# Layer 0 of a two-layer graph network: VectorE keeps a round's destinations and second harmonic in a PSUM bank

## The chip, the cores and the metric

One core of one Trainium2 chip. The metric is device time in microseconds (us) of one execution of the whole program, as a median of runs; lower is better. Engine names are those of the profile: PE is TensorE, DVE is VectorE, ACT is ScalarE, POOL is GpSimd, SP is SyncE. L653 is line 653 of the kernel before.

## The reference

Two message-passing layers over 6250 nodes and 206250 edges (sorted by destination), each followed by a residual sum and a layer norm. The change touches the edge part of the first layer only.

```python
# layer 0, for every edge e = (src, dst); es: 1 harmonic, ev: 3 harmonics
xs_e, xv_e = xs[src], xv[src]                       # gather by source
out_s = (einsum(xs_e * es, W_ss) / sqrt(64) + einsum(xv_e, ev, W_vv) * ISQ3 / sqrt(32)) * ISQ2
out_v = (einsum(xs_e, ev, W_sv) * ISQ3 / sqrt(64) + einsum(xv_e, es, W_vs) * ISQ3 / sqrt(32)) * ISQ2
messages = concat(out_s, out_v) * sigmoid(edge_scalars @ W_rad.T + b_rad)
agg = segment_sum(messages, dst, num_segments=n)    # scatter by destination
h = x + agg
...
x = layernorm(x + concat(hs @ L_s, hv @ L_v))
x = layernorm(x + second_layer(x, ...))             # another edge layer, not changed here
```

All products by the weights of layer 0 are made once per node into a table of 448 columns, so that an edge needs one gathered row, a few products by its four harmonics, sums of parts, one product by the radial part, and the scatter.

## The kernel before

**Stages.** The program makes the table of layer 0, runs edge layer 0 (about 77 to 2460 us of the profiled execution), works on the nodes, runs edge layer 1 (about 2590 to 5044 us), and norms the result. In both edge layers the edges go by in 403 supertiles of 512 edges (4 columns, TPS, of 128 edges, one to a partition). Four supertiles (SLOTS) are a round; there are 101 rounds. On each engine a loop runs over the rounds and holds the code of four supertiles; the first and the last round stand outside it.

**One supertile of layer 0, by engine.** Each engine runs its own list of instructions in order; semaphores tie them.

- POOL issues four indirect DMAs (L373), one per column; each reads 128 source numbers out of SBUF (srcs) and gathers 128 table rows into one of four slots of rows0. A slot is filled again once ACT (semaphore s_wtd) and DVE (s_wone) have used its rows.
- ACT waits for the rows, weights two parts of them by harmonics 3 and 0 (L470, eight instructions, scale from the tile harm), copies harmonics from dst_sh to harm every other supertile (L445), and makes the sigmoid of the radial product in PSUM (L498).
- DVE (function supertile): weights a third part by harmonic 1 (weight_by_one, L653, which waits for ACT's s_whead), adds a fourth part by harmonic 2 in four instructions (L660, the last of which waits for PE's sums of two supertiles ago), adds the finished sums of two supertiles ago to the node array (add_sums, L719), makes the one-hot matrix of the destinations against the current window of 128 nodes (select, L712), sums parts (L679 twice, the second waits for ACT's sigmoid) and multiplies by the radial part (L685, from PSUM). Where edges reach into a further window of nodes (444 one-hots for 401 supertiles in the stretch) it makes another one-hot and another sum (further, L739).
- PE multiplies one-hot by messages (sums, L967) into banks 4 to 6 and makes the radial product of the supertile after next (radial0, L947) into banks 0 to 3.

**Order and queues.** Between rounds DVE branches back (L785) and loads the round's windows from SBUF into registers (windows_of, L776) before it can form the addresses of the next round's instructions. Small register instructions of DVE's sequencer (named DVEq in the profile) stand between the others; they keep the engine waiting only where the sequencer has not run ahead of it. The tile dst_sh holds, for two chunks of four rounds, 16 columns of destinations and harmonics per supertile; SP reloads a chunk when DVE is through with it (s_add), so data for the next round lies there long before.

The two instructions that the change touches, and the wait at a round's start:

```python
nc.vector.tensor_tensor(u[:, :, 384:480], r[:, :, 352:448], by(1), ALU.mult)                    # L653, by(1) is a view of harm
return nc.vector.tensor_tensor(onehot[:, b, :, :], bc(iota[...], 1, [P, TPS, P]),              # L712
                               bc(dst, 2, [P, TPS, P]), ALU.is_equal)                           # dst is a view of dst_sh
if j == 0: dve.wait_ge(s_dsh[l], (i // CHUNK + 1) * 16)                                         # L755
```

Of the kernel before, what the change touches and what calls it, by code (L numbers as in the profile page):

```python
# [10 lines left out]
P = 128  # L11
TPS = 4
SUP_EDGES = TPS * P
SLOTS = 4
# [10 lines left out]
CHUNK = 4  # L25
# [29 lines left out]
def mk_gnn_resnorm_d2_gnn_r8_694f30_kernel(nc, a):  # L55
    f32, bf16, i32, i16 = mybir.dt.float32, mybir.dt.bfloat16, mybir.dt.int32, mybir.dt.int16
    ALU = mybir.AluOpType
# [3 lines left out]
    with ctx:  # L61
# [3 lines left out]
        def sem(name):  # L65
            return ctx.enter_context(nc.semaphore(name))
# [7 lines left out]
        at = SLOTS * TPS * ROW0  # L74
# [70 lines left out]
        def bank(b, n=1):  # L145
            return ps[:, b * BANK:(b + n) * BANK]
# [6 lines left out]
        wps = [two_to_a_bank(2 * b, 192) for b in range(2)]  # L153
        FIRST, MORE = 4, 6
        hps = bank(7)
        fps = [bank(6), bank(7)]

        def of_node(j, b=0, n=DIM):
# [31 lines left out]
        s_msg = [sem(f"messages_made{l}") for l in range(2)]  # L190
        s_wtd = [sem(f"rows_weighted{l}") for l in range(2)]
        s_whead = sem("scalar_parts_weighted")
        s_wone = [sem(f"rows_weighted_by_dve{l}") for l in range(2)]
        s_part = [sem(f"message_part{l}") for l in range(2)]
        s_both = sem("message_both_parts")
# [405 lines left out]
        def _(dve):  # L601
# [40 lines left out]
            def bc(x, axis, shape):  # L642
                return x.unsqueeze(axis).to_broadcast(shape)

            def weight_by_one(l, s, i, j, opens):

                def by(k):
                    return harm[:, j, :].rearrange("p (t k) -> p t k", k=4)[:, :, k:k + 1].to_broadcast([P, TPS, 96])

                if l == 0:  # L650
                    dve.wait_ge(s_whead, s + 1)
                    u, r = weighted0[:, j % DEEP0, :, :], rows0[:, j, :, :]
                    nc.vector.tensor_tensor(u[:, :, 384:480], r[:, :, 352:448], by(1), ALU.mult)  # L653
                    for t in range(TPS):
                        if t == 1:
                            dve.wait_ge(s_add[0], s + 1)
                        if t == TPS - 1 and not opens:
                            dve.wait_ge(s_agg[0], s + 1)
                        to = u[:, t, 128:224]
                        last = nc.vector.scalar_tensor_tensor(to, r[:, t, 0:96], harm[:, j, 4 * t + 2:4 * t + 3], to,  # L660
                                                              ALU.mult, ALU.add)
                else:
                    dve.wait_ge(s_wtd[1], s + 1)
                    u, r = weighted1[:, j % 2, :, :], rows1[:, j, :, :]
                    nc.vector.tensor_tensor(u[:, :, 352:448], r[:, :, 32:128], by(1), ALU.mult)  # L665
                    if not opens:
                        dve.wait_ge(s_agg[1], s + 1)
                    last = nc.vector.tensor_tensor(u[:, :, 448:544], r[:, :, 128:224], by(2), ALU.mult)  # L668
                last.then_inc(s_wone[l], 1)
# [35 lines left out]
                dve.wait_ge(s_both, s + 1)  # L705
                nc.vector.tensor_tensor(m[:, :, 64:96], h[:, :, 1, 0:MV], w[:, :, 160:192], ALU.mult).then_inc(s_msg[1], 1)  # L706

            def select(i, j, b, window):

                of_round = dst_sh[:, :, :].rearrange("p (q j) c -> p q j c", j=SLOTS)  # L710
                dst = of_round[:, bass.ds(i % (2 * CHUNK), 1), j, 0:TPS].rearrange("p o t -> p (o t)")
                return nc.vector.tensor_tensor(onehot[:, b, :, :], bc(iota[:, bass.ds(window * P, P)], 1, [P, TPS, P]),  # L712
                                               bc(dst, 2, [P, TPS, P]), ALU.is_equal)
# [7 lines left out]
            def edge_layer(l):  # L721
# [17 lines left out]
                def further(s, i, j, window, k):  # L739
# [7 lines left out]
                    at = dve.snap(window + k + 1).with_bounds(min_val=1, max_val=LAST)  # L747
                    dve.reg_mov(visit, e + 1)
                    dve.wait_ge(s_addx[l], next_visit())
                    select(i, j, 2, at).then_inc(s_ohx[l], 1)  # L750
                    dve.reg_mov(waiting_more, at)

                def supertile(s, i, j, windows, more, opens=False):
                    if j == 0:
                        dve.wait_ge(s_dsh[l], (i // CHUNK + 1) * 16)  # L755
                    weight_by_one(l, s, i, j, opens)
                    if opens:
# [4 lines left out]
                        add_sums(l, FIRST + j % 2, windows[j - 2] if j > 1 else held(of_last[j])).then_inc(s_add[l], 1)  # L762
                    if l == 0:
                        dve.wait_ge(s_wtd[0], s + 1)
                    select(i, j, j % 2, windows[j])
                    (messages0, messages1)[l](s, j)
                    with dve.If(more > 0):
                        further(s, i, j, windows[j], 0)
# [3 lines left out]
                    if j > 1:  # L772
                        dve.reg_mov(of_last[j - 2], windows[j])

                def windows_of(i):
                    return nc.values_load_multi_w_load_instructions(  # L776
                        wtab[0:1, bass.ds(i, 1), 0:2, :], engines=[dve.engine], min_val=0, max_val=LAST,
                        skip_runtime_bounds_check_because="a dst is a node's number, so its window is one of the tiles")[1]

                values = windows_of(0)  # L780
                for j in range(SLOTS):
                    if l == 0 and j == 2:
                        dve.wait_ge(s_acc0x, 16)
                    supertile(j, 0, j, values, values[SLOTS + j], opens=j < 2)
                with dve.Fori(1, ROUNDS - 1) as i:  # L785
                    values = windows_of(i)
                    for j in range(SLOTS):
                        supertile(i * SLOTS + j, i, j, values, values[SLOTS + j])
                values = windows_of(ROUNDS - 1)
                for j in range(LAST_SLOTS):  # L790
                    supertile((ROUNDS - 1) * SLOTS + j, ROUNDS - 1, j, values, values[SLOTS + j])
# [431 lines left out]
```

## Time and profile before

| what | value |
|---|---|
| median of 3 runs | 4607.15 us (4604.56 to 4610.92) |
| span of the profiled execution | 5144.5 us |
| edge layer 0 in it | 77 to 2460 us |
| edge layer 1 in it | 2590 to 5044 us |
| DVE busy, share of the span | 75% |
| POOL busy, share of the span | 67% |
| PE busy, share of the span | 83% |

The profiled execution is 537 us longer than the median run. Its page gives, for every engine, the time its instructions took and the idle time before them with what ended it; the chain of work is followed back from the last instruction through whatever released each step. Durations of neighbouring DVE instructions overlap a little, so the step from one start to the next is what an instruction costs in a row.

### The profile page before, as it was taken

To read this page: it belongs to the slowest core of one execution; us is meant where nothing else is said; L and a number is where in the kernel's file an instruction comes from. 1 tells how busy PE (TensorE), PEld (TensorE's weight loads), DVE (VectorE), ACT (ScalarE), POOL (GpSimd) and SP (SyncE) were. 2 spreads that over 40 slices of the span, in tenths; PEclk is the share of its full clock that TensorE was granted. 3 is DMA by queue.
4 is the path that set the end of the run, shared out by engine and by line. 5 is a ranking of instruction groups with operands and counts; after the bars stand their busy time and mean duration, and the time that the engine had idled before them with its cause. 6 is when DMAs were issued, how large, how long until landed. Compare 5 with 4: busy or idle time off the path is not lost.

```text
span 5144.5 us, 61111 instructions
## 1 busy us (share of the span) xinstructions
PE 4277.3 (83%) x12412; PEld 2600.5 (51%) x12413; DVE 3878.0 (75%) x8785; ACT 2612.5 (51%) x8195; POOL 3471.2 (67%) x3267
## 2 busy tenths in 40 slices
PE   6877877877877887887878888988988898888897
PEld 4555555555555555555644444444444444444445
DVE  5878877877878887887667777777777776777777
ACT  3545555545555555554544445545454454555554
POOL 4777777777777777777266666666666666666661
PEclk7555555555555555555889999999998899999999
DMA  7655565665565665656233333333333333333331
GB/s 250 167 166 160 166 171 159 166 169 160 167 168 161 168 167 164 168 162 166 85 85 88 84 86 84 87 82 86 87 86 82 84 84 83 87 86 85 85 86 52
DMA packets 245761, 640.14 MB, mean 124 GB/s; under 512 B 57085, under 2 KB 95407, under 8 KB 245627
## 3 DMA queue, kind: packets, MB, share of 16 engines
q0 software_dynamic: 181152, 556.66, 39.8%
q1 hardware_dynamic: 64576, 83.11, 5.3%
q8 instruction: 13, 0.21, 0.0%
q14 instruction: 20, 0.16, 0.0%
HBM read 618.66 MB, written 20.88 MB: 124 GB/s over the span
## 4 chain that ended last, share of the span: by engine, by line
DVE 34%; PE 27%; issue 16%; another core or an unknown queue 9%; ACT 6%; DVEq 4%; DMA 2%; POOL 2%; ACTq 0%; POOLq 0%; SPq 0%
PE ps L967 15%; DVE work L679 10%; PE ps L960 6%; DVE work L660 6%; DVE onehot L712 5%; ACT work L470 5%; PE ps L954 3%; DVE work L653 2%; DVE acc L719 2%; POOL arena L373 2%; DVE arena L719 1%; PE ps L947 1%; DVE work L699 1%; DVEq L776 1%
## 5 line engine op out<-in xcount | busy, mean ns | idle before, releaser
L373 POOL DMA_INDIRECT work<-table,srcs x1596 | 1639.5, 1027 | 796.7 <-issue 633.8
L373 POOL DMA_INDIRECT arena<-table,srcs x1596 | 1755.0, 1100 | 611.4 <-issue 516.3
L967 PE MATMUL ps<-arena,onehot 128*128 128x161 f32 x3608 | 1034.6, 464 | 507.4 <-DVE arena L685 264.4
L967 PE MATMUL ps<-work,onehot 128*128 128x384 f32 x3608 | 1345.2, 521 | 79.3 <-DVE work L706 59.1
L967 PEld LDWEIGHTS ps<-arena,onehot 128*128 128x128 f32 x3608 | 884.8, 308 | 830.3 <-issue 769.8
L470 ACT ACTIVATE work<-arena,harm 128x160 f32<-128x160 f32 (+1 forms) x3224 | 984.7, 389 | 301.0 <-DMA arena<-table,srcs 266.3
L470 ACT ACTIVATE work<-work,harm 128x96 f32<-128x96 f32 (+1 forms) x3224 | 1070.3, 415 | 22.2 <-DMA work<-table,lists 11.6
L967 PEld LDWEIGHTS ps<-work,onehot 128*128 128x128 f32 x3608 | 684.8, 199 | 631.8 <-issue 270.6
L947 PE MATMUL ps<-wrad,escal 49*128 49x320 f32 x1612 | 905.2, 707 | 0.0
L960 PE MATMUL ps<-fc,hid 128*128 128x384 f32 x1612 | 639.1, 522 | 219.2 <-ACT hid L560 124.5
L679 DVE TENSOR_REDUCE work<-work 128x256 f32<-128x768 f32 (+1 forms) x806 | 656.7, 853 | 149.6 <-ACT ps L498 85.4
L560 ACT ACTIVATE hid<-ps 128x256 f32<-128x256 f32 x403 | 153.6, 381 | 1182.3 <-remote 652.7
L498 ACT ACTIVATE ps<-ps 128x640 f32<-128x640 f32 x403 | 276.5, 686 | 824.2 <-issue 285.2
L712 DVE TENSOR_TENSOR onehot<-iota,dst_sh 128x512 f32 (+1 forms) x902 | 616.9, 684 | 15.5 <-issue 6.4
L947 PEld LDWEIGHTS ps<-wrad,escal 49*128 49x128 f32 x1612 | 427.7, 293 | 262.4 <-issue 247.8
L960 PEld LDWEIGHTS ps<-fc,hid 128*128 128x128 f32 x1612 | 315.4, 201 | 482.5 <-ACT hid L560 162.7
L660 DVE SCALAR_TENSOR_TENSOR work<-arena,harm,work 128x96 f32<-128x96 f32 x1612 | 405.9, 311 | 171.6 <-remote 137.3
L668 DVE TENSOR_TENSOR work<-work,harm 128x384 f32<-128x384 f32 x403 | 223.1, 554 | 322.0 <-remote 189.5
L665 DVE TENSOR_TENSOR work<-work,harm 128x384 f32<-128x384 f32 x403 | 223.7, 555 | 280.1 <-issue 146.5
L703 DVE TENSOR_TENSOR work<-work,ps 128x768 f32<-128x768 f32 x403 | 380.4, 944 | 0.0
L685 DVE TENSOR_TENSOR arena<-work,ps 128x640 f32<-128x640 f32 x403 | 330.8, 821 | 13.9
L653 DVE TENSOR_TENSOR work<-arena,harm 128x384 f32<-128x384 f32 x403 | 223.2, 554 | 152.8 <-issue 109.3
(127 smaller groups left out, 2503.9 us busy)
## 6 DMA issues: line engine op xcount, KB each, us to landing
escal<-in_escal SPq DMA_DIRECT2D x404, 98.0 KB
arena<-table,srcs POOLq DMA_INDIRECT x1596
work<-table,srcs POOLq DMA_INDIRECT x1596
table<-work SPq DMA_DIRECT2D x49, 224.0 KB, 4.6
dst_sh<-in_dst_sh SPq DMA_DIRECT2D x52, 160.0 KB
table<-work SPq DMA_DIRECT2D x7, 784.0 KB, 4.0
acc<-in_xd SPq DMA_DIRECT2D x1, 3920.0 KB
arena<-in_xd SPq DMA_DIRECT2D x7, 560.0 KB, 4.6
```

The costliest lines, as they stand in the source:

```text
L373: pool.indirect_dma_start(out=rows[:, j, t, :], out_offset=None, in_=table, in_offset=bass.IndirectOffsetOnAxis(ap=of[:, j, t:t + 1], axis ...
L470: last = nc.scalar.activation(u[:, t, to:to + c1 - c0], r[:, t, c0:c1], ACT.Copy, scale=harm[:, j, at:at + 1])
L498: nc.scalar.activation(rad[j % 2], rad[j % 2], ACT.Sigmoid).then_inc(s_act[0], 1)
L653: nc.vector.tensor_tensor(u[:, :, 384:480], r[:, :, 352:448], by(1), ALU.mult)
L660: last = nc.vector.scalar_tensor_tensor(to, r[:, t, 0:96], harm[:, j, 4 * t + 2:4 * t + 3], to, ALU.mult, ALU.add)
L679: return nc.vector.tensor_reduce(to, parts[:, :, :, 0:MS].rearrange("p t k c -> p t c k"), AX.X, ALU.add)
L685: nc.vector.tensor_tensor(m[:, :, 0:DIM], u[:, :, 0:DIM], c, ALU.mult).then_inc(s_msg[0], 1)
L703: nc.vector.tensor_tensor(blocks(m[:, :, 192:384], 3), blocks(u[:, :, 256:544], 3)[:, :, :, 0:MS], bc(w[:, :, 64:128], 2, [P, TPS, 3, MS]) ...
L712: return nc.vector.tensor_tensor(onehot[:, b, :, :], bc(iota[:, bass.ds(window * P, P)], 1, [P, TPS, P]), bc(dst, 2, [P, TPS, P]), ALU.is_ ...
L947: last = mm(rad[j % 2][:, 2 * k:2 * k + 2, :], escal[:, j, k * P:(k + 1) * P], wrad[:], start=True, stop=True)
L960: last = mm(wps[j % 2][:, 2 * k:2 * k + 2, :], hid[:, j % 2, k * P:(k + 1) * P], fc2[:], start=True, stop=True)
L967: last = mm(bank(to)[:, 0:(MSG0, MSG1)[l]], onehot[:, b, t, :], m[:, j % 2, t, :], start=t == 0, stop=t == TPS - 1)
```

## The change

In layer 0, DVE copies the 16 destinations (as floats) and the 16 second harmonics (harmonic 1) of each partition for the next round from dst_sh into two halves of PSUM bank 7, which nothing else uses in layer 0. It does so at the end of each round, before the loop's branch (and once before the first round). The one-hots, first and further, read the destination from there, and L653's product reads the harmonic from there. The wait for dst_sh at a round's start becomes a wait for these copies, and the wait for dst_sh moves in front of them. ACT's copies into harm stay, since L470 and L660 still use them. Layer 1 is as it was.

```diff
+        dst_ps = bank(7)[:, 0:2 * SLOTS * TPS].rearrange("p (b j t) -> p b j t", b=2, j=SLOTS)
+        harm_ps = bank(7)[:, 2 * SLOTS * TPS:4 * SLOTS * TPS].rearrange("p (b j t) -> p b j t", b=2, j=SLOTS)
...
+            def of_psum(x, i, j):
+                return x[:, bass.ds(i & 1, 1), j, :].rearrange("p o t -> p (o t)")
...
-                    nc.vector.tensor_tensor(u[:, :, 384:480], r[:, :, 352:448], by(1), ALU.mult)
+                    nc.vector.tensor_tensor(u[:, :, 384:480], r[:, :, 352:448], bc(of_psum(harm_ps, i, j), 2, [P, TPS, 96]), ALU.mult)
...
-            def select(i, j, b, window):
+            def hold(i):
+
+                of_round = dst_sh[:, :, :].rearrange("p (q j) c -> p q j c", j=SLOTS)[:, bass.ds(i % (2 * CHUNK), 1), :, :]
+                first = of_round.rearrange("p o j c -> p (o j) c")
+                nc.vector.tensor_copy(dst_ps[:, bass.ds(i & 1, 1)].rearrange("p o j t -> p (o j) t"), first[:, :, 0:TPS])
+                sh1 = first.bitcast(f32)[:, :, TPS:5 * TPS].rearrange("p j (t k) -> p j t k", k=4)[:, :, :, 1]
+                nc.vector.tensor_copy(harm_ps[:, bass.ds(i & 1, 1)].rearrange("p o j t -> p (o j) t"), sh1).then_inc(s_held, 1)
+
+            def select(l, i, j, b, window):
+
+                if l == 0:
+                    return nc.vector.tensor_tensor(onehot[:, b, :, :], bc(iota[:, bass.ds(window * P, P)], 1, [P, TPS, P]),
+                                                   bc(of_psum(dst_ps, i, j), 2, [P, TPS, P]), ALU.is_equal)
...
-                    if j == 0:
+                    if j == 0 and l == 0:
+                        dve.wait_ge(s_held, i + 1)
+                    if j == 0 and l == 1:
                         dve.wait_ge(s_dsh[l], (i // CHUNK + 1) * 16)
...
+                def hold_next(i):
+
+                    dve.wait_ge(s_dsh[0], ((i + 1) // CHUNK + 1) * 16)
+                    hold(i + 1)
...
                 with dve.Fori(1, ROUNDS - 1) as i:
                     values = windows_of(i)
                     for j in range(SLOTS):
                         supertile(i * SLOTS + j, i, j, values, values[SLOTS + j])
+                    if l == 0:
+                        hold_next(i)
```

The instructions of DVE move at two places. ISA and REGISTER_ALU are register instructions of its sequencer. The end of a round in the loop of layer 0, after the code for further windows, before the change:

```order
L751 ISA
L770 COMPARE_AND_BRANCH
L769 UNCONDITIONAL_BRANCH
L773 ISA
L785 COMPARE_AND_BRANCH
```

The same place after the change:

```order
L791 UNCONDITIONAL_BRANCH
L795 ISA
L720 ISA [waits dst_sh_loaded0]
L720 REGISTER_ALU
L720 ISA
L720 COPY ps<-dst_sh 128x16
L722 ISA
L722 COPY ps<-dst_sh 128x16
L817 REGISTER_ALU
L817 COMPARE_AND_BRANCH
```

Five sequencer instructions (three ISA and two REGISTER_ALU) and the two copies stand there more. The start of a round, from the branch back to the first product and what follows it, before the change:

```order
L785 ISA
L776 TENSOR_LOAD wtab
L755 ISA
L651 ISA [waits dst_sh_loaded0]
L653 TENSOR_TENSOR work<-arena,harm 128x4x96 [waits scalar_parts_weighted]
L660 SCALAR_TENSOR_TENSOR work<-arena,harm,work 128x96
```

And after it:

```order
L817 ISA
L803 TENSOR_LOAD wtab
L775 REGISTER_ALU
L659 ISA [waits dst_and_harmonic_in_psum]
L661 REGISTER_ALU [waits scalar_parts_weighted]
L661 ISA
L661 TENSOR_TENSOR work<-arena,ps 128x4x96
L668 SCALAR_TENSOR_TENSOR work<-arena,harm,work 128x96
```

The wait for dst_sh is gone from here, one for the copies stands in its place, and two more register instructions stand between the load of the windows and the product.

## Rows read from the trace of the kernel before

**Rows 1.** Stretches: us; busy us of PE, PEld, DVE, ACT, POOL; granted clock, DMA share.

```profile
77.00:2460.00 2383.00, 1883.98 (x5182) 1303.32 (x5183) 1899.85 (x4104) 1259.79 (x3915) 1764.27 (x1605) 0.57 0.60 167
2590.00:5044.00 2454.00, 2158.97 (x5971) 1115.63 (x5972) 1794.91 (x4090) 1225.30 (x3899) 1653.07 (x1610) 0.93 0.32 85
```

**Rows 2.** Chain that ended last, 1200 to 1500 us: shares; longest pieces (start, us, what).

```profile
by line: DVE work L679 22.7%; issue 21.5%; DVE work L660 13.2%; DVE onehot L712 8.8%; another core or an unknown queue 8.6%; DVE work L653 5.8%; DVE acc L719 4.1%; POOL arena L373 3.4%; DVEq L776 2.1%; DMA arena<-table,srcs 2.1%; ACT work L
...
1254.55 8.42 issue
1341.74 13.31 another core or an unknown queue
```

**Rows 3.** Waits, 77 to 2460 us: who waited for whom, us, times, longest.

```profile
DVE work L660 <- remote: 137.3, 24, 12.5
DVE work L653 <- issue: 109.3, 121, 3.9
...
DVE work L679 <- ACT ps L498: 85.4, 13, 9.1
...
DVE work L653 <- ACT work L470: 30.7, 25, 12.7
```

**Rows 4.** Groups, 77 to 2460 us: line engine op tiles shapes xcount | busy, mean ns | idle.

```profile
L373 POOL DMA_INDIRECT arena<-table,srcs x1596 | 1755.0, 1100 | 611.4 <-issue 516.3 <-DVE work L660 89.7 <-ACT work L470 5.5
...
L660 DVE SCALAR_TENSOR_TENSOR work<-arena,harm,work 128x96 f32<-128x96 f32 x1604 | 403.9, 311 | 171.6 <-remote 137.3 <-PE ps L967 26.6 <-issue 7.6
L685 DVE TENSOR_TENSOR arena<-work,ps 128x640 f32<-128x640 f32 x401 | 329.2, 821 | 13.9
L712 DVE TENSOR_TENSOR onehot<-iota,dst_sh 128x512 f32 x444 | 303.7, 684 | 7.7 <-DVE acc L719 5.2 <-issue 2.6
...
L653 DVE TENSOR_TENSOR work<-arena,harm 128x384 f32<-128x384 f32 x401 | 222.1, 554 | 152.8 <-issue 109.3 <-ACT work L470 30.7 <-DMA acc<-in_xd 12.4
L719 DVE TENSOR_TENSOR acc<-acc,ps 128x161 f32 x447 | 140.6, 315 | 0.0
```

**Rows 5.** Timeline, POOL, 1509 to 1516 us: start, us, instruction, [idle before <-releaser].

```profile
1508.40 0.95 POOL L373 DMA_INDIRECT arena<-table,srcs  x1 [0.31 <-issue]
1509.65 1.31 POOL L373 DMA_INDIRECT arena<-table,srcs  x1 [0.30 <-issue]
1511.26 1.45 POOL L373 DMA_INDIRECT arena<-table,srcs  x1 [0.30 <-issue]
```

**Rows 6.** Timeline, VectorE, from 1503 us: a round's end, then one supertile.

```profile
1503.28 0.82 DVE L685 TENSOR_TENSOR arena<-work,ps 128x640 f32<-128x640 f32 x1
1504.96 0.56 DVE L653 TENSOR_TENSOR work<-arena,harm 128x384 f32<-128x384 f32 x1 [0.85 <-issue]
...
1508.85 0.82 DVE L685 TENSOR_TENSOR arena<-work,ps 128x640 f32<-128x640 f32 x1
1509.59 0.55 DVE L653 TENSOR_TENSOR work<-arena,harm 128x384 f32<-128x384 f32 x1
...
1511.20 0.69 DVE L712 TENSOR_TENSOR onehot<-iota,dst_sh 128x512 f32 x1
```

**Rows 7.** Timeline, 1541 to 1544 us: TensorE comes late, and a gather beside L685.

```profile
1541.61 0.69 ACT L498 ACTIVATE ps<-ps 128x640 f32<-128x640 f32 x1 [10.60 <-remote]
...
1543.01 0.95 POOL L373 DMA_INDIRECT arena<-table,srcs  x1 [0.30 <-issue]
1543.05 0.82 DVE L685 TENSOR_TENSOR arena<-work,ps 128x640 f32<-128x640 f32 x1
```

**Rows 8.** Lines L776, L755, L651, 1503 to 1505 us: ns min/median/max, start.

```profile
L776 DVEq TENSOR_LOAD <-wtab x1: 626/626/626, 1504.0 to 1504.0; - x1
...
L755 DVEq FUSED_REGOPS  x1: 119/119/119, 1504.7 to 1504.7; - x1
...
L651 DVEq FUSED_REGOPS  x1: 60/60/60, 1504.9 to 1504.9; - x1
```

**Rows 9.** Groups, POOL, 2590 to 5044 us (layer 1).

```profile
L373 POOL DMA_INDIRECT work<-table,srcs x1596 | 1639.5, 1027 | 796.7 <-issue 633.8 <-DVE work L668 138.6 <-ACT work L470 22.9
```

More of the change, by code:

```diff
@@ L192, in mk_gnn_resnorm_d2_gnn_r8_694f30_kernel @@
         s_whead = sem("scalar_parts_weighted")
+        s_held = sem("dst_and_harmonic_in_psum")
         s_wone = [sem(f"rows_weighted_by_dve{l}") for l in range(2)]
@@ L749, in further @@
                     dve.wait_ge(s_addx[l], next_visit())
-                    select(i, j, 2, at).then_inc(s_ohx[l], 1)
+                    select(l, i, j, 2, at).then_inc(s_ohx[l], 1)
                     dve.reg_mov(waiting_more, at)
                 def supertile(s, i, j, windows, more, opens=False):
-                    if j == 0:
+                    if j == 0 and l == 0:
+                        dve.wait_ge(s_held, i + 1)
+                    if j == 0 and l == 1:
                         dve.wait_ge(s_dsh[l], (i // CHUNK + 1) * 16)
@@ L764, in supertile @@
                         dve.wait_ge(s_wtd[0], s + 1)
-                    select(i, j, j % 2, windows[j])
+                    select(l, i, j, j % 2, windows[j])
                     (messages0, messages1)[l](s, j)
@@ L778, in windows_of @@
                         skip_runtime_bounds_check_because="a dst is a node's number, so its window is one of the tiles")[1]
+                if l == 0:
+                    dve.wait_ge(s_dsh[0], 16)
+                    hold(0)
                 values = windows_of(0)
@@ L784, in edge_layer @@
                     supertile(j, 0, j, values, values[SLOTS + j], opens=j < 2)
+                if l == 0:
+                    hold_next(0)
                 with dve.Fori(1, ROUNDS - 1) as i:
@@ L788, in edge_layer @@
                         supertile(i * SLOTS + j, i, j, values, values[SLOTS + j])
+                    if l == 0:
+                        hold_next(i)
                 values = windows_of(ROUNDS - 1)
```

## The prediction

> **What bounds the kernel now.** First I read where the time lies. The two edge layers take 2383 and 2454 us of the 5144.5 us span [rows 1]; the change touches the first only, so every sum below is one of its 403 supertiles and 101 rounds. There VectorE (DVE) is busy for 1900 us and GpSimd (POOL) for 1764 us; TensorE (PE) is granted 0.57 of its clock on the mean, so it is at the lower of its two levels (1.2 GHz) for most of that layer, and at 0.93 in the second [rows 1].
>
> Busy shares don't say who sets the end, and here they mislead. POOL looks saturated: its gathers are busy for 1755.0 us and idle before them for 611.4 us, together 2366 of 2383 us, and most of that idle time is the constant 0.30 us between two gathers [rows 4, 5]. And its gathers are held up by DVE. A gather takes 0.95 us where nothing disturbs it, 1.31 us where it starts just after L653 and 1.45 us where it starts just after the one-hot L712; each ends about 0.82 us after the DVE instruction does (L653 from 1509.59 for 0.55, gather to 1510.96; L712 from 1511.20 for 0.69, gather to 1512.71) [rows 5, 6]. Both of these instructions read two operands from SBUF. A gather that starts under L685, which reads one from SBUF and one from PSUM, takes 0.95 us [rows 7]. So the mean of 1100 ns against 0.95 us is 0.15 us of hold, 1596 times, 239 us in the layer [rows 4].
>
> The Trainium skill has the rule (SBUF — State Buffer, Who interferes with whom): a DVE instruction with two SBUF inputs contends with a GpSimd instruction that reads SBUF, one with at most one does not. The trace agrees, by the three durations above. What the rule promises by itself is rival 1.
>
> But the chain of waits doesn't run through POOL. From 1200 to 1500 us it goes over DVE's instructions one behind another (L679, L660, L712, L653, L719), and POOL has 3.4% of it, the landing of rows 2.1% [rows 2]. DVE's own waits say the same: it waited for rows, by way of ACT, for 30.7 us in the whole layer, but 137.3 us at L660 (which waits for PE's sums) and 85.4 us at L679 (PE's radial product, by way of ACT) [rows 3]. These come in blocks: every hundred us or so PE's results come late by some ten us, as at 1541.61, where ACT had waited 10.60 us [rows 7], or in the two long pieces of the chain [rows 2]. In such a block POOL goes on and fills all four row slots; after it DVE lives on that stock. So POOL is nearly always at work, and still seldom what DVE waits for. In the profiled execution DVE's list, with PE's late blocks in it, sets the pace.
>
> **What the change takes away.** L653 (401 times) and L712 (444 times) no longer read two operands from SBUF. If nothing else is held, POOL gains up to 239 us. On the path this is worth what DVE waits for rows: 30.7 us [rows 3]. Bounds: 0 if these waits stem from the landing alone, and (3.4% + 2.1%) of 2383 us, 131 us, if all that the chain gives to POOL and to landings goes [rows 1, 2]. I take 31 us, since it is DVE's own wait. What is late next is DVE itself, or PE's sums at the lower clock. L660, with two SBUF operands in four instructions of 311 ns, goes on holding gathers [rows 4].
>
> **What it does to the two instructions.** Durations with an operand in PSUM are there: L685 takes 821 ns for 640 elements, L653 554 ns for 384, L712 684 ns for 512 [rows 4]. From L653 to L685 that is 267 ns for 256 elements, from L653 to L712 130 ns for 128: 1.04 and 1.02 ns an element, so PSUM adds nothing to be seen. Nearer still, from start to next start L685 costs 0.74 us [rows 6]. I take zero; the bounds are -5 and +10 ns an instruction, 845 times, -4 to +9 us.
>
> The Trainium skill speaks against this (VectorE: DVE Perf Modes, The TRN2 errata): it gives an instruction 58 cycles beside its elements with SBUF as the source, and 120 with PSUM. An estimate from that page is 65 ns more for each of 845 instructions, 55 us, and the sum would be 80 us of loss in place of 25. The rows above disagree with it for two-operand products. It is rival 3.
>
> **What it adds.** Per round DVE gets two copies of 16 elements and seven more register instructions: five before the branch, two after the load of the windows (the order before and after shows them). They stand at the one spot where DVE's sequencer is not ahead of its engine: at a round's start L653 begins 1.68 us after L685 did, where inside a round it is 0.74 us, and the engine is idle for 0.85 us [rows 6]. The sequencer is then busy with the branch, the load (626 ns) and two register instructions, which lie between the load's end at 1504.65 and L653 at 1504.96, so 0.15 us each with what surrounds them; their own durations are 60 and 119 ns [rows 6, 8]. So seven cost 0.42 us (60 ns each) to 1.05 us (0.15 us each); I take 0.7 us, 0.10 us each, since those before the branch can run partly under L685, as the branch does now. The copies have no like in the trace. The nearest row, L719, has 161 elements and takes 315 ns [rows 4]; two of 16 elements take no longer, so 0 to 0.63 us, and I take zero, since the 0.85 us of idle engine hides them. If the sequencer caught up, that cover would go, and they would cost 0.2 to 0.6 us. The new wait for the copies has nothing to wait for: they end before the load of the windows does. Behind it stand L653 and all of DVE, and behind DVE PE's sums (s_msg) and POOL's refill (s_wone).
>
> How many of the 100 round ends are on the path? The load L776 is in 2.1% of the chain, 6.3 us of 300 us, which at 626 ns is 10 loads; 300 us hold 12.6 rounds of 23.8 us [rows 2, 8]. So 80%. The loss is 100 x 0.8 x 0.7 = 56 us; bounds 100 x 0.8 x 0.42 = 34 us and 100 x 1.68 = 168 us. Inside a round one more register instruction stands before each product by the harmonic; it runs under L685's 0.74 us, and costs at most 0.15 us behind the 48 further one-hots, 7 us, which I leave at nothing.
>
> SP, ACT and PE keep their lists, and no DMA is added or moved. The data that the copies wait for were loaded rounds before.
>
> **The sum.** 56 - 31 + 0 = +25 us on the span of 5144.5 us, +1.0% of the layer. The median run is 537 us shorter than that span, and where these lie no view says. I carry the 25 us over as they are: 4607 + 25 = 4632 us.
>
> **Rivals.**
>
> 1. *POOL paces the unprofiled run* (faster). If PE's late blocks are smaller without the profiler, POOL has no time to catch up. Its list in layer 0 is then 1755 + 1596 x 0.30 = 2234 us; DVE's is 1900 us busy and 109.3 us at the round starts, 2009 us [rows 3, 4]. For it: the blocks would be a large part of the missing 537 us. Against it: the same reckoning over both layers (1755.0 + 1639.5 us of gathers, 3192 x 0.30 us, and 307 us of the span outside the edge layers) gives 4659 us, more than the median of 4607 [rows 4, 9], so unprofiled gathers must be cheaper than the trace shows them, and how much cheaper decides. If only by those 52 us, half of them here, layer 0 took 2208 us and would then take DVE's 2009 + 56 = 2065 us: a gain of 143 us, 4464 us. If by 0.14 us a gather (223 us), POOL is level with DVE, and nothing is gained. Midway: 4536 us. This is also the skill's rule on shared ports taken alone.
> 2. *A wash.* The round's end costs its lower bound (34 us) and the relief is the waits for rows: 4607 + 3 = 4610 us; or POOL and DVE are level, and what one gains the other loses.
> 3. *PSUM reads are slow* (slower still). A one-hot reads one PSUM element 128 times in a row, which no row shows. Beside its elements (1.04 ns each) L719 has a fixed part of 315 - 167 = 148 ns [rows 4]; if such a read cost half of that again, 845 x 0.074 = 63 us come on top: 4695 us. Against it stand L685 and L719 themselves. The skill's estimate would put this rival at 4687 us.
> 4. *The holds move.* Gathers freed from L653 and L712 run into L660 instead, and the relief is half: 4607 + 56 - 15 = 4648 us.
>
> Rival 1 decides the sign: from the point where POOL's unprofiled list is longer than about 2065 us, the change gains.
>
> **How the numbers follow.** Forecast (DVE's list is longer by its round ends): 0.40, 4617 to 4665 us. Rival 1: 0.37. Rival 2: 0.15. Rival 3: 0.04. Rival 4: 0.04. About 0.2% (9 us) is what a measurement of this kernel can tell from no change. Slower: 0.40 + 0.04 + 0.04 - 0.02 (for the forecast's lower edge) = 0.46; faster 0.37 and the lower edge of the wash, 0.38; same 0.16. The range leaves out the lower quarter of rival 1 and rival 3: 4530 to 4668 us.
>
> **What would show it.** In the trace after: gathers of layer 0 at a mean near 0.97 us in place of 1.10; the one-hot and the product at 684 and 554 ns within 10 ns; the idle time before the first product of a round at about 1.5 us in place of 0.85; L776's successor still in some 2% of the chain; POOL's waits for used rows up by some 200 us. The forecast is wrong if DVE's waits for rows prove to have been more than 60 us in runs without the profiler, or if the sequencer does its seven instructions under L685.

## The result, and the profile after

The changed kernel takes 4507.79 us (median of 4 runs, 4504.23 to 4509.35) against 4607.96 us before (4604.56 to 4610.92): ratio 0.9783, 95% interval 0.9769 to 0.9796. It is faster by 100 us. The forecast was 4632 us in a range of 4530 to 4668: the sign was wrong, and the time lies below the range.

The profiled execution of before that stands ahead of the prediction was a disturbed one, so the same kernel was profiled again. The second profile spans 4610.2 us, as the timed runs do, and from here on "before" means that one. The page of the changed kernel (span; TensorE's granted clock in 40 slices; chain by engine):

```profile
span 4505.5 us, 62204 instructions
...
PEclk8555555565655655555789999999999999999998
...
DVE 43%; PE 13%; issue 13%; ACT 9%; DMA 8%; POOL 7%; DVEq 6%; ACTq 0%; SPq 0%; POOLq 0%
```

Stretches of before, one for each edge layer: from, to and length in us, busy us of PE, PEld, DVE, ACT, POOL with the number of instructions, granted clock, DMA share, GB/s.

```profile
70.00:2283.00 2213.00, 1884.51 (x5189) 1294.64 (x5187) 1912.97 (x4103) 1262.98 (x3918) 1715.83 (x1612) 0.57 0.64 180
2409.00:4512.00 2103.00, 2027.88 (x5997) 1078.88 (x5996) 1802.51 (x4106) 1243.84 (x3917) 1611.97 (x1612) 0.99 0.36 99
```

The same of after:

```profile
70.00:2171.00 2101.00, 1856.07 (x5169) 1285.83 (x5170) 1912.95 (x4291) 1255.03 (x3908) 1525.49 (x1611) 0.58 0.68 189
2304.00:4410.00 2106.00, 2023.10 (x5994) 1076.67 (x5994) 1802.28 (x4106) 1241.51 (x3918) 1614.97 (x1612) 0.99 0.37 99
```

These answer to [rows 1]. The first layer is 112 us shorter, the second is 3 us longer, and the clock stays at 0.57 to 0.58, most of the layer at the lower of its two levels (1.2 GHz). So the gain lies in the layer that was changed. Measured from the first gather to the last, layer 0 takes 2213 us before and 2103 after.

Groups in layer 0 before (line, engine, operation, tiles, shapes, count; busy us, mean ns; idle us before them, and what ended it):

```profile
L373 POOL DMA_INDIRECT arena<-table,srcs x1596 | 1700.4, 1065 | 492.3 <-issue 418.3 <-DVE work L660 68.6 <-ACT work L470 5.5
...
L712 DVE TENSOR_TENSOR onehot<-iota,dst_sh 128x512 f32 x444 | 304.3, 685 | 7.7 <-DVE acc L719 7.7
...
L653 DVE TENSOR_TENSOR work<-arena,harm 128x384 f32<-128x384 f32 x401 | 224.2, 559 | 282.9 <-ACT work L470 253.8 <-issue 14.3 <-DMA acc<-in_xd 13.8
```

The same in after, with line numbers as they are now (L378 was L373, L661 was L653, L668 was L660, L687 was L679, L693 was L685, L727 was L712, L739 was L719, L475 was L470; L720 and L722 are the two copies):

```profile
L378 POOL DMA_INDIRECT arena<-table,srcs x1596 | 1511.7, 947 | 571.2 <-issue 556.6 <-ACT work L475 14.3 <-DVE work L668 0.3
...
L727 DVE TENSOR_TENSOR onehot<-iota,ps 128x512 f32 x444 | 301.9, 680 | 7.8 <-DVE acc L739 7.8
...
L661 DVE TENSOR_TENSOR work<-arena,ps 128x384 f32<-128x384 f32 x400 | 219.7, 549 | 170.2 <-issue 139.3 <-ACT work L475 15.7 <-DMA acc<-in_xd 14.6
...
L722 DVE COPY ps<-dst_sh x98 | 18.6, 190 | 0.0
L720 DVE CAST ps<-dst_sh x98 | 17.2, 176 | 1.4
```

These answer to [rows 4]. A gather's mean falls from 1065 to 947 ns. Reading an operand in PSUM lengthens neither instruction: the one-hot takes 680 ns for 685, the product 549 for 559.

Waits before in layer 0 (who waited for whom: us, times, longest):

```profile
ACT work L470 <- DMA arena<-table,srcs: 889.8, 387, 5.3
...
DVE work L653 <- ACT work L470: 253.8, 316, 12.9
```

And after:

```profile
DVE work L661 <- issue: 139.3, 98, 1.5
...
DVE work L661 <- ACT work L475: 15.7, 2, 12.7
```

These answer to [rows 3], and they are the heart of the case. In the second profile of before, VectorE waited 253.8 us for rows, by way of ScalarE, where [rows 3] has 30.7. After the change 15.7 us of that are left, and its long wait is for nothing but its own sequencer, 98 times 1.4 us: the round ends.

The chain of waits from 1200 to 1500 us says the same. Before:

```profile
by line: POOL arena L373 26.4%; issue 19.8%; DMA arena<-table,srcs 19.8%; DVE work L660 9.9%; DVE work L679 7.2%; ACT work L470 5.9%; DVE onehot L712 2.7%; DVEq L776 1.9%; DVE work L653 1.8%; DVE acc L719 1.7%; DVEq L785 0.4%; DVEq L755 0.4
```

After:

```profile
by line: DVE work L687 30.0%; DVE work L668 18.7%; issue 14.8%; DVE onehot L727 11.7%; DVE work L661 6.2%; DVE acc L739 5.2%; DVEq L803 3.0%; DVEq L727 1.8%; DVEq L661 1.5%; DVE arena L693 1.3%; DVEq L720 1.1%; DVEq L795 0.8%; DVEq L659 0.7
```

This answers to [rows 2], where POOL had 3.4%. In the second profile of before, the chain goes through gathers (26.4%) and their landings (19.8%); after, both are gone from it, and it goes over VectorE's list.

One hold, seen directly. Timeline of before (start, us, engine, line), a gather that starts just after the one-hot:

```profile
1510.52 0.69 DVE L712 TENSOR_TENSOR onehot<-iota,dst_sh 128x512 f32 x1
1510.58 1.44 POOL L373 DMA_INDIRECT arena<-table,srcs  x1 [0.30 <-DVE work L660]
```

It takes 1.44 us and ends 0.81 us after the one-hot, as in [rows 5, 6]. The same meeting in after:

```profile
1519.76 0.68 DVE L727 TENSOR_TENSOR onehot<-iota,ps 128x512 f32 x1
...
1519.87 0.94 POOL L378 DMA_INDIRECT arena<-table,srcs  x1 [0.30 <-issue]
```

0.94 us. I counted the gathers from 1000 to 1600 us that took over 1.1 us. Before: 125 of 438, 99 of them started under the one-hot and 26 under the product. After: none of 461.

The price is at the round's end. VectorE's timeline there in after:

```profile
1526.62 0.82 DVE L693 TENSOR_TENSOR arena<-work,ps 128x640 f32<-128x640 f32 x1
1527.35 0.18 DVE L720 CAST ps<-dst_sh  x1
1527.52 0.19 DVE L722 COPY ps<-dst_sh  x1
1529.14 0.55 DVE L661 TENSOR_TENSOR work<-arena,ps 128x384 f32<-128x384 f32 x1 [1.43 <-issue]
```

This answers to [rows 6]. From L693 to the next round's first product it is 2.52 us, where it was 1.68.

### The profile page after: what moved, and what is told of

Read it like the earlier page. It is cut to its first block, busy times and chain, and to the rows that moved or that the text cites. A ratio compares the mean times of both kernels' runs of the same rounds, so it can differ in the third digit from the quotient of the medians.

```text
span 4505.5 us, 62204 instructions
## 1 busy us (share of the span) xinstructions
PE 4110.7 (91%) x12412; PEld 2543.8 (56%) x12413; DVE 3897.2 (86%) x8987; ACT 2620.2 (58%) x8195; POOL 3186.9 (71%) x3267
## 4 chain that ended last, share of the span: by engine, by line
DVE 43%; PE 13%; issue 13%; ACT 9%; DMA 8%; POOL 7%; DVEq 6%; ACTq 0%; SPq 0%; POOLq 0%
DVE work L687 14%; DVE work L668 8%; PE ps L1001 8%; ACT work L475 8%; DMA work<-table,srcs 7%; POOL work L378 7%; DVE onehot L727 5%; DVE work L661 3%; DVE acc L739 2%; DVE work L676 2%; PE ps L994 2%; DVE onehot L732 2%; DVEq L803 2%; DVE arena L739 1%; PE ps L988 1%
## 5 line engine op out<-in xcount | busy, mean ns | idle before, releaser
L378 POOL DMA_INDIRECT work<-table,srcs x1596 | 1599.2, 1002 | 486.5 <-issue 453.8
L378 POOL DMA_INDIRECT arena<-table,srcs x1596 | 1511.7, 947 | 571.2 <-issue 556.6
L1001 PE MATMUL ps<-work,onehot 128*128 128x384 f32 x3608 | 1281.5, 501 | 78.9 <-DVE onehot L732 60.6
L475 ACT ACTIVATE work<-work,harm 128x96 f32<-128x96 f32 (+1 forms) x3224 | 1071.7, 415 | 454.0 <-DMA work<-table,srcs 441.4
L475 ACT ACTIVATE work<-arena,harm 128x160 f32<-128x160 f32 (+1 forms) x3224 | 984.9, 389 | 83.9 <-DVE arena L693 66.5
L1001 PEld LDWEIGHTS ps<-work,onehot 128*128 128x128 f32 x3608 | 657.0, 191 | 595.8 <-issue 148.4
L981 PE MATMUL ps<-wrad,escal 49*128 49x320 f32 x1612 | 894.3, 700 | 0.0
L687 DVE TENSOR_REDUCE work<-work 128x256 f32<-128x768 f32 (+1 forms) x806 | 655.2, 854 | 0.5
L994 PE MATMUL ps<-fc,hid 128*128 128x384 f32 x1612 | 588.0, 488 | 7.8 <-ACT hid L565 7.8
L673 DVE TENSOR_TENSOR work<-work,harm 128x384 f32<-128x384 f32 x403 | 224.8, 558 | 286.0 <-ACT work L475 273.1
L668 DVE SCALAR_TENSOR_TENSOR work<-arena,harm,work 128x96 f32<-128x96 f32 x1612 | 405.9, 313 | 0.0
L661 DVE TENSOR_TENSOR work<-arena,ps 128x384 f32<-128x384 f32 x403 | 221.4, 549 | 170.9 <-issue 139.3
L693 DVE TENSOR_TENSOR arena<-work,ps 128x640 f32<-128x640 f32 x403 | 330.9, 821 | 13.9
L732 DVE TENSOR_TENSOR onehot<-iota,dst_sh 128x512 f32 (+1 forms) x451 | 309.3, 686 | 7.8 <-DVE arena L739 7.8
L727 DVE TENSOR_TENSOR onehot<-iota,ps 128x512 f32 (+1 forms) x451 | 306.7, 680 | 7.8 <-DVE acc L739 7.8
```

What stands on the lines that cost most here:

```text
L378: pool.indirect_dma_start(out=rows[:, j, t, :], out_offset=None, in_=table, in_offset=bass.IndirectOffsetOnAxis(ap=of[:, j, t:t + 1], axis ...
L475: last = nc.scalar.activation(u[:, t, to:to + c1 - c0], r[:, t, c0:c1], ACT.Copy, scale=harm[:, j, at:at + 1])
L687: return nc.vector.tensor_reduce(to, parts[:, :, :, 0:MS].rearrange("p t k c -> p t c k"), AX.X, ALU.add)
L693: nc.vector.tensor_tensor(m[:, :, 0:DIM], u[:, :, 0:DIM], c, ALU.mult).then_inc(s_msg[0], 1)
L981: last = mm(rad[j % 2][:, 2 * k:2 * k + 2, :], escal[:, j, k * P:(k + 1) * P], wrad[:], start=True, stop=True)
L994: last = mm(wps[j % 2][:, 2 * k:2 * k + 2, :], hid[:, j % 2, k * P:(k + 1) * P], fc2[:], start=True, stop=True)
```

## The experiments

**Theory H**: in the timed runs of before GpSimd's gathers paced layer 0, VectorE's two-operand reads held them, and taking the holds away is the gain. Rival **L**: TensorE's late blocks, which only the first profile shows, are part of the kernel, and the gain comes from them. Rival **P**: the gain comes from what the copies do beside, packed operands or instructions at another place, and not from where they lie. When H had held, a second question was left, why both halves alone are faster than the whole. **Theory E**: with the holds gone VectorE's list paces the layer, and the work added at the round's end is what it costs. Rival **G**: GpSimd still paces, by its gathers at their unheld length. Rival **C**: the copies cost their engine time wherever they stand.

Times of all runs; "layer 0" is from the first gather to the last in the profile of the run, "round end" the median, from 200 to 2000 us, of the distance from L693's start to the next round's first product. Each group of runs had runs of before beside it: their median is 4607.96 us beside after, 4610.88 beside the halves and the copies in SBUF, and 4601.88 beside the last three. So times of different groups are compared by their ratios, or by layer 0.

| kernel | median us | ratio to before, 95% | gather ns | round end us | layer 0 us |
|---|---|---|---|---|---|
| before, again | 4612.06 (one run) | | 1065 | 1.69 | 2213 |
| after | 4507.79 | 0.9783 (0.9769 to 0.9796) | 947 | 2.52 | 2103 |
| one-hot only | 4470.70 | 0.9696 (0.9680 to 0.9713) | 967 | 2.14 | 2067 |
| harmonic only | 4488.85 | 0.9734 (0.9717 to 0.9750) | 985 | 2.36 | 2090 |
| copies in SBUF | 4615.39 | 1.0011 (1.0002 to 1.0021) | 1065 | 2.52 | 2214 |
| copies twice | 4530.79 | 0.9849 (0.9833 to 0.9865) | 947 | 2.78 | 2128 |
| copies mid-round | 4450.29 | 0.9675 (0.9659 to 0.9691) | 951 | 1.83 | 2050 |
| one-hot only, mid-round | 4451.68 | 0.9675 (0.9659 to 0.9692) | 966 | 1.62 | 2056 |

### The kernel before, profiled again

No edit.

> The kernel before, unaltered, profiled once more. Theory H (the holds of gathers paced layer 0, and the late blocks of TensorE in the first profile belong to that one execution): a span of 4600 to 4615 us, no wait of ACT for TensorE above 6 us in layer 0, layer 0 about 100 us longer than the 2103 us of the changed kernel, gathers of layer 0 at a mean of 1.04 to 1.10 us, VectorE waiting for rows for about 100 us or more. Rival L (the late blocks are part of the kernel, and the change shortened them): late blocks of 10 us are there again in the profile.

The rows of it stand above. TensorE's late blocks, the 137.3 and 85.4 us of [rows 3], aren't there, nor in any of the seven other profiles. L falls. What made them in the first execution wasn't tried. That first trace is also short of records: it holds 28043 updates of semaphores, and the second 67579. A wait is put down to its cause by these records, so the first trace gives the causes of waits, and the chain in [rows 2], only in part. Idle time doesn't depend on them. Before L660 it is 171.6 us in the first profile [rows 4], before L679 149.6 us, and both are 0.0 in the second, so the blocks cost VectorE some 320 us there and not only the 223 us that have a named cause. The line of the first page:

```profile
L679 DVE TENSOR_REDUCE work<-work 128x256 f32<-128x768 f32 (+1 forms) x806 | 656.7, 853 | 149.6 <-ACT ps L498 85.4
```

### Copies into SBUF

```diff
-        dst_ps = bank(7)[:, 0:2 * SLOTS * TPS].rearrange(...)
-        harm_ps = bank(7)[:, 2 * SLOTS * TPS:4 * SLOTS * TPS].rearrange(...)
+        held_sb = sb("held_sb", [P, 4 * SLOTS * TPS])
+        dst_ps = held_sb[:, 0:2 * SLOTS * TPS].rearrange(...)
+        harm_ps = held_sb[:, 2 * SLOTS * TPS:4 * SLOTS * TPS].rearrange(...)
```

> The changed kernel with the two copies into a tile in SBUF in place of the PSUM bank: the same instructions in the same order, but the one-hots and the product read two operands from SBUF again. Theory H: the holds are back, so 4600 to 4650 us, gathers of layer 0 at a mean of 1.04 to 1.10 us. Rival P (the shift, or the packed copies themselves): 4508 us.

4615.39 us, ratio 1.0011: no gain is left. Groups of this kernel in layer 0, up to 2120 us:

```profile
L379 POOL DMA_INDIRECT arena<-table,srcs x1477 | 1575.3, 1067 | 456.4 <-issue 397.9 <-DVE work L669 47.2 <-ACT work L476 11.0
...
L728 DVE TENSOR_TENSOR onehot<-iota,held_sb 128x512 f32 x413 | 283.0, 685 | 7.4 <-DVE acc L740 7.4
```

Its waits there:

```profile
DVE work L662 <- ACT work L476: 193.7, 195, 12.5
```

The gathers are back at 1067 ns up to 2120 us, 1065 over the whole layer (118 of 440 over 1.1 us), and so are VectorE's waits for rows. Instructions, their order and the round's end (2.52 us) are those of after; only the memory of the copies differs. P falls. The Trainium skill's rule on two inputs in SBUF (SBUF — State Buffer, Who interferes with whom) agrees with this pair of kernels: the one-hot takes 685 ns here and 680 in after, and what differs is the gather beside it. And the longer round end costs next to nothing here, because VectorE waits for rows behind it in any case.

### One half alone

One-hot only: the product reads SBUF as before, one copy is left.

```diff
-   nc.vector.tensor_tensor(u[:, :, 384:480], r[:, :, 352:448], bc(of_psum(harm_ps, i, j), 2, [P, TPS, 96]), ALU.mult)
+   nc.vector.tensor_tensor(u[:, :, 384:480], r[:, :, 352:448], by(1), ALU.mult)
...
-   nc.vector.tensor_copy(harm_ps[...], sh1).then_inc(s_held, 1)
```

> The changed kernel, but only the one-hots read PSUM; L653's product reads harm in SBUF as before, and one copy per round is left. Theory H: the one-hots' holds, about two thirds of all, are gone, GpSimd's list is close to VectorE's: 4505 to 4535 us, gathers of layer 0 at a mean of 0.98 to 1.01 us. Rival P (a longer round end shifts VectorE against GpSimd, and that is the gain): 4508 us as well, but with gathers at 0.95 us. Rival L: 4508 us, gathers no clue.

4470.70 us, better than expected. Its gathers up to 2120 us:

```profile
L378 POOL DMA_INDIRECT arena<-table,srcs x1583 | 1530.5, 967 | 499.6 <-issue 487.4 <-ACT work L475 11.6 <-DVE work L668 0.6
```

VectorE's timeline at a round's end:

```profile
1523.37 0.82 DVE L693 TENSOR_TENSOR arena<-work,ps 128x640 f32<-128x640 f32 x1
1524.10 0.17 DVE L720 CAST ps<-dst_sh  x1
1525.52 0.56 DVE L661 TENSOR_TENSOR work<-arena,harm 128x384 f32<-128x384 f32 x1 [1.24 <-issue]
```

Harmonic only: the one-hot reads SBUF as before, one copy is left.

```diff
-   nc.vector.tensor_copy(dst_ps[...], first[:, :, 0:TPS])
...
-                if l == 0:
+                if False:
                     return nc.vector.tensor_tensor(onehot[:, b, :, :], ...
```

> The changed kernel, but only the product by the second harmonic reads PSUM; the one-hots read their destinations in dst_sh as before, and one copy per round is left. Theory H: a third of the holds is gone: 4550 to 4580 us, gathers of layer 0 at a mean of 1.01 to 1.05 us. Rival P (the shift at the round's end): 4508 us.

4488.85 us, better than expected too. Its gathers and its longest waits of VectorE:

```profile
L378 POOL DMA_INDIRECT arena<-table,srcs x1565 | 1542.0, 985 | 488.1 <-issue 479.2 <-ACT work L475 7.3 <-DVE work L668 1.2
```

```profile
DVE work L661 <- issue: 138.0, 97, 1.4
...
DVE work L661 <- ACT work L475: 15.6, 2, 12.7
```

Either half takes most of the holds away: 98 of the 118 ns without the one-hot's, 80 without the product's, and not in the proportion of the 99 and 26 meetings counted before. The count shows it: with the one-hot's holds gone 19 of 469 gathers are over 1.1 us, all under the product, where it was 26; with the product's gone 44 of 464, all under the one-hot, where it was 99. So the remaining instruction is met less often. That the gathers now start elsewhere in the supertile, since VectorE no longer waits for them, is my reading, and no run tests it. That is what I missed in both expectations, which priced the holds one by one. And both kernels beat the whole change because their round ends are shorter: 2.14 and 2.36 us for 2.52. Over 100 rounds that is 38 and 16 us, and layer 0 is shorter by 36 and 13. Harmonic only lacks one copy and one register instruction in front of it. One-hot only lacks, beside these, the two register instructions that stand before the product in after; the two kernels differ at the round's end by these, 0.22 us. This led to theory E.

### Copies moved to the middle of a round

The wait and both copies stand behind the one-hot of the round's second supertile.

```diff
                     select(l, i, j, j % 2, windows[j])
+                    if holds:
+                        hold_next(i)
...
-                        supertile(i * SLOTS + j, i, j, values, values[SLOTS + j])
-                    if l == 0:
-                        hold_next(i)
+                        supertile(i * SLOTS + j, i, j, values, values[SLOTS + j], holds=l == 0 and j == 1)
```

> The changed kernel, with the wait for dst_sh and the two copies for the next round moved from the round's end to a place behind the second supertile's one-hot, where VectorE's engine has work queued. Theory E (with the holds gone VectorE's list paces layer 0, and the round's end, 2.53 us from L685's start to the next product in the trace of the changed kernel against 1.68 before, is what was added to it): the round's end falls back to 1.7 to 2.0 us, layer 0 from 2103 to 2020 to 2050 us, 4425 to 4455 us in all. Rival G (GpSimd still paces layer 0): 4500 to 4510 us. Rival C (the copies' time on the engine is the cost, wherever they stand): 4490 to 4500 us.

4450.29 us. By the ratios (0.9675 and 0.9783) that is 50 us below the change as it was made, and layer 0 is 53 us shorter; with the next run it is the fastest. VectorE's timeline, first a round's end, then the copies:

```profile
1509.36 0.82 DVE L693 TENSOR_TENSOR arena<-work,ps 128x640 f32<-128x640 f32 x1
1511.18 0.56 DVE L661 TENSOR_TENSOR work<-arena,ps 128x384 f32<-128x384 f32 x1 [1.00 <-issue]
...
1518.53 0.67 DVE L727 TENSOR_TENSOR onehot<-iota,ps 128x512 f32 x1
1519.12 0.17 DVE L720 CAST ps<-dst_sh  x1
1519.20 0.17 DVE L722 COPY ps<-dst_sh  x1
1519.29 1.61 DVE L687 TENSOR_REDUCE work<-work 128x256 f32<-128x768 f32 x2
```

Gathers up to 2120 us:

```profile
L378 POOL DMA_INDIRECT arena<-table,srcs x1596 | 1518.5, 951 | 511.6 <-issue 492.5 <-ACT work L475 17.7 <-DVE work L668 1.5
```

The round's end is 1.83 us, 0.15 us above that of before, and the copies move what follows by 0.16 us: the second product sum L687 starts 0.76 us after the one-hot, where it is 0.60 in other supertiles. C, which had them cost the same everywhere, falls, and so does G, which had 4500 to 4510 us. By E, layer 0 should be 69 us shorter than after's by its round ends and 16 us longer by the copies: 2050 us, as measured.

The same with the one-hot alone (the edits of "one-hot only" and this one together):

> Only the one-hots read PSUM, and their one copy stands behind the second supertile's one-hot. Theory E: VectorE's list is as short as in the run with both copies there or a little shorter, but GpSimd still has the holds of L653's product (gathers at 0.97 us, 1612 x (0.967 + 0.304) = 2049 us): 4445 to 4460 us, little better than the 4470.7 us with that copy at the round's end. Rival G: 4470 us.

4451.68 us, the same within the intervals. Its round end is shorter still (1.62 us), but now GpSimd's list is the longer one (2049 us to 2021 in the table below): VectorE's waits up to 2120 us,

```profile
DVE work L661 <- ACT work L475: 72.8, 84, 12.5
DVE work L661 <- issue: 43.9, 52, 1.0
```

are 72.8 us for rows, where mid-round with both copies has 15.9. Behind this step there is nothing more to be had from round ends; here the case of G has come.

### Copies made twice

A second pair of copies into other columns of the bank, which nothing reads, ahead of the pair at the round's end.

```diff
+   nc.vector.tensor_copy(dst_ps2[...], first[:, :, 0:TPS])
+   sh1 = first.bitcast(f32)[...]
+   nc.vector.tensor_copy(harm_ps2[...], sh1)
    nc.vector.tensor_copy(dst_ps[...], first[:, :, 0:TPS])
```

> The changed kernel with both copies made twice per round at the round's end, the second pair into other columns of the same bank that nothing reads. Theory E: the round's end grows by another 0.6 to 0.8 us, 60 to 80 us in all: 4565 to 4590 us. Rival G: 4505 to 4515 us, since GpSimd would hide it.

4530.79 us: in the direction of E, but layer 0 is only 25 us longer than after's, where I expected 60 to 80. G, which had no more than 4515 us, falls here too. VectorE's timeline at a round's end:

```profile
1504.03 0.82 DVE L695 TENSOR_TENSOR arena<-work,ps 128x640 f32<-128x640 f32 x1
1504.77 0.17 DVE L722 CAST ps<-dst_sh  x1
1504.93 0.19 DVE L724 COPY ps<-dst_sh  x1
1505.06 0.18 DVE L725 CAST ps<-dst_sh  x1
1505.19 0.19 DVE L727 COPY ps<-dst_sh  x1
1506.80 0.55 DVE L663 TENSOR_TENSOR work<-arena,ps 128x384 f32<-128x384 f32 x1 [1.41 <-issue]
```

The second pair adds 0.26 us; the idle time behind it stays at 1.41 us. It brought two register instructions with it, one before each copy (lines L725 and L727: ns min/median/max, first and last start), while the wait and the other register instructions are made once for both pairs. So the edit was smaller than the expectation took it to be, which priced the whole addition a second time.

```profile
L725 DVEq FUSED_REGOPS  x1: 65/65/65, 1505.0 to 1505.0; - x1
L727 DVEq FUSED_REGOPS  x1: 65/65/65, 1505.1 to 1505.1; - x1
```

100 x 0.26 = 26 us, and layer 0 is longer by 25.

### Two lists, and the longer one sets the layer

E with H gives a reckoning that can be held against every run. GpSimd's list is its 1612 instructions in the layer (the stretches above), nearly all of them gathers, each with the mean of a gather and the 0.30 to 0.31 us that lie between two in its timeline (I take 0.305). VectorE's list is that of after, 2103 us, with 100 round ends of their own length in place of 2.52 us, and the mid-round copies at 16 us (8 for one). For before the round end is the 1.68 us of [rows 6].

| kernel | GpSimd's list | VectorE's list | longer | layer 0 measured |
|---|---|---|---|---|
| before | 2208 | 2019 | 2208 | 2213 |
| copies in SBUF | 2208 | 2103 | 2208 | 2214 |
| after | 2018 | 2103 (set) | 2103 | 2103 |
| one-hot only | 2050 | 2065 | 2065 | 2067 |
| harmonic only | 2079 | 2087 | 2087 | 2090 |
| copies twice | 2018 | 2129 | 2129 | 2128 |
| copies mid-round | 2025 | 2050 | 2050 | 2050 |
| one-hot only, mid-round | 2049 | 2021 | 2049 | 2056 |

All within 7 us. VectorE's list was set from one run (after), so that row proves nothing; the other seven do. The gathers' mean and the round end of each row come from that kernel's own trace, so the table is an account of the times and not a forecast of them.

## Why the prediction was wrong, step by step

**What paces the layer.** This is the step that failed. "In the profiled execution DVE's list, with PE's late blocks in it, sets the pace" fits that execution, but not the second one, which is as long as the timed runs: there GpSimd's list paces the layer. The late blocks let GpSimd catch up, and so hid that VectorE lives on GpSimd's rows; and the chain of [rows 2], with its 3.4% for POOL, was followed through a trace that is short of records. The profile had what was needed to see it: its span was 537 us above the median, so something in it was not in the timed runs, and the late blocks were a candidate in plain view. Without their 137.3 and 85.4 us [rows 3], the layer's 2383 us leave 2160, and without all 321 us of idle time before L660 and L679 2062; GpSimd's list in the same trace was 2234 us. With the blocks gone VectorE would be through before GpSimd is, and GpSimd sets the pace. I had all of these numbers, but kept that trace as it was for the sum and put the other case among the rivals.

**The relief, 31 us.** By the two lists it is 2208 - 2019 = 189 us, six times that. The 31 us were VectorE's waits for rows in the first trace; in the second they are 253.8, and the prediction's own mark for being wrong was 60. Lost records explain little of the 30.7: all idle time before L653 was 152.8 us in the first trace [rows 4] and 282.9 in the second.

**The reads in PSUM, zero.** Right: 680 ns against 685 and 549 against 559. Rival 3 is out. The Trainium skill's 62 cycles more for a source in PSUM (VectorE: DVE Perf Modes, The TRN2 errata) don't show in either instruction.

**The round's end, 0.7 us each, 80 of 100 on the path.** The term was too small by a third: 2.52 - 1.68 = 0.84 us each, and all of them count. L803, the load of the windows, has 3.0% of the chain from 1200 to 1500 us, 9 us, which at the 647 ns of the one looked at below is 14 loads, one for each round in that stretch. So 84 us for 56: 14 us by the size of one round end, 14 by their number. The sequencer is late at two places, by the medians of the rounds: the branch (L817) starts 1.01 us after L693 does, where it was 0.30 (L785 after L685), and the rest of the 0.84 us lies behind the load of the windows. By the two halves the two register instructions before the product cost 0.22 us, 0.11 each, near the 0.10 taken. Zero for the copies is nearly right: they run right behind L693, and the sequencer's next instruction starts 0.02 us after a copy does and doesn't wait for its end. The second pair's 0.26 us, less two register instructions at 0.11, leaves 0.04 us for two copies (an estimate); the runs don't divide the 0.84 us further. Lines L720 and L803 (the copy of the destinations and the load of the windows) at one round's end of after (ns min/median/max, first and last start):

```profile
L720 DVEq FUSED_REGOPS  x2: 76/102/127, 1527.0 to 1527.2; - x2
L720 DVEq ALU_OP  x1: 45/45/45, 1527.2 to 1527.2; - x1
```

```profile
L803 DVEq TENSOR_LOAD <-wtab x1: 647/647/647, 1528.1 to 1528.1; - x1
```

**The sum.** With the measured sizes it is 84 - 189 + 0 = -105 us, the difference of the two longer lists (the 189 uses the 84, so this doesn't test each by itself). Layer 0 fell by 110, the kernel by 100. All its terms were there; the relief was read from the wrong execution.

**Rival 1** was the case that came, with 2208 us before and 2065 after; it was 2213 and 2103. That 2208 came out so near is in part luck, since it took half of an unexplained 52 us for layer 0. Its 2065 was 38 us short: VectorE was busy for 1913 us, not 1900, and idle for 52 us more that I hadn't counted (15.7 and 14.6 at L661, 13.8 at L693, 7.8 at L727), while its idle time at the round starts was 139 us, not 109 + 56. I gave it 0.37 because its reckoning over both layers came out longer than the median. That spoke against gathers as long as in the trace, not against GpSimd: in the second profile they are shorter in both layers, 1065 ns for 1100 and 1000 for 1027.

**Rival 4** (the holds move into L660, now L668) is out: of 78 gathers that start under L668 between 1000 and 1600 us in after, the longest takes 1.03 us and half of them 0.95. So L668 holds a gather by 0.08 us at most there, and by 0.13 us at most in the mid-round run.

**The signs.** Gathers at 947 ns (0.97 us foretold), idle before the first product 1.43 us (1.5), L803 3.0% of the chain (2%). GpSimd's idle time before gathers rose by 79 us only, from 492.3 to 571.2, where 200 was foretold: the layer got shorter by most of what the gathers gave up.

## What to carry to other kernels

When a profiled execution is longer than the timed runs, find what is in it that can't be in them, take it out, and compare the engines' lists with the layer that remains before reading any wait. A stage is as long as its longest list, so a relief is worth the distance down to the next list, and a change that also lengthens that next list pays for it in full. Small instructions at a loop's end, where the sequencer isn't ahead of its engine, cost 0.84 us a round here, and 0.31 us (0.15 + 0.16) from the middle of the round; try the move before dropping them.

## What the runs showed of the hardware

A gather's issue on GpSimd (0.94 to 0.95 us alone) that is held by a VectorE instruction with both operands in SBUF ends 0.81 to 0.83 us after that instruction does, whatever its length: so for all held gathers from 1000 to 1600 us in the second profile of before, in after, in both halves, with the copies in SBUF and with the copies mid-round. With one operand in PSUM, at the same place, it takes 0.94 us, and under the sums of parts (L679, one operand) none of 115 took over 0.96 us. The cost isn't the sum over such instructions: with the product's holds gone, 44 of 464 gathers are held under the one-hot where 99 of 438 were, with the one-hot unchanged. A copy of 16 elements from SBUF to PSUM takes 0.17 to 0.19 us, and a second pair of them, with two register instructions, costs 0.26 us at the round's end. What made TensorE late in blocks in one execution of before, by some 320 us of VectorE's time in that layer, stays open; that the same trace lost more than half of its semaphore records makes the profiling itself a suspect, which no run here tests.
